# Position products of a disentangled attention: two thirds of them moved to two 64-row tiles of TensorE

## The reference

```python
c2p = jnp.einsum('bhsd,hkd->bhsk', q, pos_k)
c2p = jnp.take_along_axis(c2p, clip(rel + span), axis=-1)
p2c = jnp.einsum('bhsd,hkd->bhsk', k, pos_q)
p2c = jnp.take_along_axis(p2c, clip(-rel + span), axis=-1)
scores = scores + c2p / bias_scale + p2c.swapaxes(-1, -2) / bias_scale
```

## Time and profile before

| | |
|---|---|
| median of 3 executions | 1429.16 us (1428.75 to 1429.78) |
| the profiled execution | 1423.23 us |
| its span in the trace | 1421.4 us |
| prelude's first fill to first `t1` | 428.40 to 445.47 us |
| the 31 units with fills | 445.47 to 1186.44 us |
| one unit in the middle | 23.75 us |
| TensorE busy in that unit | 23.28 us |
| VectorE, ScalarE, GpSimd busy in it | 18.54, 15.01 and 11.14 us |

### The profile page before, as it was taken

The page is one execution under the profiler, slowest core; times in us unless marked ns, Lnnn a source line. Parts: engine busy times, 40 slices in busy tenths (PEclk is TensorE's granted clock), DMA queues, the critical chain, the costliest instruction groups (busy, mean ns, idle before and its releaser), DMA issues. The chain is left out here.

```text
span 1421.4 us, 31237 instructions
## 1 busy us (share of the span) xinstructions
PE 1111.4 (78%) x9281; PEld 990.6 (70%) x9281; DVE 963.6 (68%) x2968; ACT 698.2 (49%) x1449; POOL 553.3 (39%) x418
## 2 busy tenths in 40 slices
PE   4990521885617999999999999999999998730886
PEld 3980411885406898989898989888888886620886
DVE  6887742665635877777777777777777776630564
ACT  2435410443534666666666666666666664210443
POOL 0007135553003444444444444444444443026454
PEclk9995555998668999999999999999999999655999
DMA  5900053223198355555565555555555540043221
GB/s 142 228 15 0 1 195 113 77 78 99 41 312 202 103 142 136 142 134 141 135 139 137 139 137 138 138 138 138 134 142 136 140 111 1 1 162 106 64 80 50
DMA packets 75273, 165.91 MB, mean 117 GB/s; under 512 B 8249, under 2 KB 54784, under 8 KB 66528
## 3 DMA queue, kind: packets, MB, share of 16 engines
q1 hardware_dynamic: 69600, 152.75, 42.0%
q0 software_dynamic: 5632, 12.67, 2.6%
HBM read 130.76 MB, written 35.67 MB: 117 GB/s over the span
## 5 line engine op out<-in xcount | busy, mean ns | idle before, releaser
L1143 POOL TENSOR_SCALAR ds_scores<-ds_scores,ds_max 128x256 f32<-128x256 f32 x256 | 349.0, 1363 | 393.0 <-DVE ds_max L1335 392.9
L1327 DVE TENSOR_TENSOR ds_p2c<-ds_bank,ds_p2c 128x512 f32<-128x512 f32 x256 | 175.8, 687 | 93.1 <-PE ds_bank L1180 93.1
L1276 ACT ACTIVATE all_xt<-ds_bank 128x512 f32<-128x512 f32 x256 | 153.0, 598 | 148.2 <-PE ds_bank L1198 148.2
L1171 PE MATMUL ds_bank<-ds_qr,ds_tab 128*128 128x128 f32 x1536 | 190.2, 278 | 32.2 <-DVE ds_qr L1311 30.0
L1171 PEld LDWEIGHTS ds_bank<-ds_qr,ds_tab 128*128 128x128 f32 x1536 | 181.9, 194 | 33.4 <-issue 33.3
L1171 PE MATMUL ds_bank<-ds_kr,ds_tab 128*128 128x128 f32 x1536 | 197.7, 275 | 0.6 <-ACT ds_p2c L1260 0.6
L1260 ACT ACTIVATE ds_c2p_t<-ds_bank 128x512 f32<-128x512 f32 x256 | 152.7, 597 | 88.6 <-PE ds_bank L1171 87.4
L1335 DVE CUSTOM_DVE_ANT_0 ds_scores<-ds_bank,ds_p2c 128x256 f32<-128x256 f32 x512 | 195.2, 417 | 0.2 <-DVE ds_p2c L1327 0.2
L1171 PEld LDWEIGHTS ds_bank<-ds_kr,ds_tab 128*128 128x128 f32 x1536 | 184.0, 192 | 1.2 <-issue 1.1
L1260 ACT ACTIVATE ds_p2c<-ds_bank 128x512 f32<-128x512 f32 x256 | 149.3, 597 | 53.4 <-PE ds_bank L1171 53.3
L1180 PE MATMUL ds_bank<-all_constants,ds_c2p_t 128*128 128x128 f32 x1024 | 157.6, 276 | 0.0
(11 more groups left out here) (245 smaller groups left out, 1746.7 us busy)
## 6 DMA issues: line engine op xcount, KB each, us to landing
ds_qr<-scratch_qk SPq DMA_DIRECT2D x32, 1024.0 KB, 11.2
ds_kr<-scratch_qk SPq DMA_DIRECT2D x32, 1024.0 KB, 13.9
ds_tab<-scratch_tables SPq DMA_DIRECT2D x64, 248.0 KB, 9.2
slots_in<-all_zero SPq DMA_DIRECT2D x2, 5160.0 KB, 38.0
ds_qs<-scratch_q_parts SPq DMA_DIRECT2D x32, 288.0 KB
ds_ks<-scratch_k_parts SPq DMA_DIRECT2D x32, 288.0 KB
0fe_xb<-slots_in SPq DMA_DIRECT2D x40, 129.0 KB, 2.1
1fe_xb<-slots_in SPq DMA_DIRECT2D x40, 129.0 KB, 2.1
```

Of the source, the lines that this page charges most:

```text
L1143: pool.tensor_scalar(S[b % NS][:, 1, :], S[b % NS][:, 1, :], mx[:, 2 * b + 1:2 * b + 2], None, ALU.subtract).then_inc(s_sub1, 1)
L1171: last = pe.matmul(pb[n % 2][:, a * P:(a + 1) * P], TAB[half][:, kind, c:c + P], mov[:, :].rearrange("p (b g s) -> p g b s", b=HALF, s=16) ...
L1276: act.activation(PT[b], pt2[:, :].rearrange("p (k s) -> p k s", k=2), ACT.Exp).then_inc(s_exp, 1)
L1327: dve.tensor_tensor(z, pt1[b % 2][:, :].rearrange("p (a k) -> p a k", a=2), z, ALU.add).then_inc(s_z, 1)
```

## The change

The twelve near fills become six double fills, each of two banks. A matmul for side 0 and group g uses the same table columns as one for side 1 and group g + 8. For `RUNS` 1 and 2 of each kind (four of the six double fills) these two are done together: for each of the 4 groups, tile 0 takes partitions 0 to 63 of the table and of the moving operand, with places 8 to 15 of both groups, tile 1 partitions 64 to 127 with places 0 to 7. Each has 2 x 8 x 8 = 128 moving columns. Tile 0 writes to bank 0, tile 1 to bank 1. The number of fp32 matmuls stays 4 x 2 = 8 in such a double fill. The third run of each kind pairs groups whose columns differ, and is done with the whole array as before. Below, P is a double fill in two row tiles and F one with the whole array.

A double fill waits until the copies of all earlier fills are done, where before the last one could be open. ScalarE copies a P with four copies of 256 columns, in runs of 8 elements, where there were two of 512 columns in runs of 16. `SHARE` is 1, 1, 1, 1, 1, 1, 2, 2: steps 0 to 5 have P, P, F, P, P, F, steps 6 and 7 two far fills each. `CONTENT_FILLS` goes from 13 to 14.

```diff
-        FILLS = near[:10] + [far[0], near[10], far[1], near[11], far[2], far[3]]
-        CONTENT_FILLS = 1 + max(n for n, f in enumerate(FILLS) if f[0] == 0)
+        RUNS = (((0, 0, 4), (1, 8, 4)), ((0, 4, 4), (1, 12, 4)), ((0, 8, 4), (1, 4, 4)))
+        FILLS = [("near", kind, runs) for kind in range(2) for runs in RUNS] + \
+                [("far", kind, (0, QUADS - 1)) for kind in range(2)] + [("far", kind, (1, 0)) for kind in range(2)]
+        FILLS = FILLS[:6] + [FILLS[6], FILLS[8], FILLS[7], FILLS[9]]
+        BANKS = [2 if f[0] == "near" else 1 for f in FILLS]
+        FIRST = [sum(BANKS[:n]) for n in range(len(FILLS))]
+        BM = sum(BANKS)
+        CONTENT_FILLS = FIRST[8]
-        SHARE = [2, 2, 2, 1, 2, 2, 2, 3]
+        SHARE = [1, 1, 1, 1, 1, 1, 2, 2]
...
-                pe.wait_ge(s_be, f + 1)
+                pe.wait_ge(s_be, f + BANKS[n])
...
+                if where[1][1] != where[0][1] + 8:
+                    for r, (side, grp, _) in enumerate(where):
+                        for a in range(4):
+                            c = TABLE - SEQ + P * side - 16 * (grp + a)
+                            last = pe.matmul(pb[r][:, a * P:(a + 1) * P], TAB[half][:, kind, c:c + P],
+                                             mov[:, :].rearrange("p (b g s) -> p g b s", b=HALF, s=16)[:, grp + a, :, :], start=True, stop=True)
+                        last.then_inc(s_bm, 1)
+                    return
+                side, grp, _ = where[0]
                 for a in range(4):
+                    c = TABLE - SEQ + P * side - 16 * (grp + a)
+                    for tile in range(2):
+                        rows = slice(tile * 64, (tile + 1) * 64)
+                        own = mov[rows, :].rearrange("p (b q g h s) -> p h q g b s", b=HALF, q=2, h=2, s=8)[:, 1 - tile, :, grp + a, :, :]
+                        last = pe.matmul(pb[tile][:, :].rearrange("p (r a n) -> p r a n", r=2, a=4)[:, :, a, :], TAB[half][rows, kind, c:c + P],
+                                         own, start=True, stop=True)
+                        if a == 3:
+                            last.then_inc(s_bm, 1)
...
+                for tile in range(2):
+                    act.wait_ge(s_bm, done + tile + 1)
+                    at = 0
+                    for side, grp, count in where:
+                        dst = to[:, side, :, :].rearrange("p b (g h s) -> p h g b s", h=2, s=8)[:, 1 - tile, grp:grp + count, :, :]
+                        last = act.activation(dst, pb[tile][:, at * 64:(at + count) * 64].rearrange("p (g b s) -> p g b s", g=count, b=HALF), ACT.Copy)
+                        at += count
+                    last.then_inc(s_be, 1)
```

More of the change, by code:

```diff
@@ L1152, in fill @@
             def fill(head, half, n):
-                kind, quad, side = FILLS[n]
-                f = (2 * head + half) * BM + n
+                what, kind, where = FILLS[n]
+                f = (2 * head + half) * BM + FIRST[n]
                 if n == 0:
@@ L1159, in fill @@
                 pe.wait_ge(s_masked, 2 * (2 * head + half) + kind + 1)
-                pe.wait_ge(s_be, f + 1)
+                pe.wait_ge(s_be, f + BANKS[n])
                 mov = (QR, KR)[kind][half]
-                if is_far(quad, side):
+                if what == "far":
+                    side, quad = where
                     pe.wait_ge(s_stack[half], 16 * 4 * (head + 1))
-                    pe.matmul(pb[n % 2][:, :], ENDS[half][:, kind, side * FAR:(side + 1) * FAR],
+                    pe.matmul(pb[FIRST[n] % 2][:, :], ENDS[half][:, kind, side * FAR:(side + 1) * FAR],
                               (QS, KS)[kind][half][:, :].rearrange("p (b s) -> p b s", b=HALF)[:, :, quad * 64:(quad + 1) * 64],
@@ L1167, in fill @@
                     return
-                for a in range(4):
[L1169 to L1174, removed]
+                if where[1][1] != where[0][1] + 8:
[7 more added lines that the diff above has]
+                side, grp, _ = where[0]
+                for a in range(4):
+                    c = TABLE - SEQ + P * side - 16 * (grp + a)
[6 more added lines that the diff above has]
+                            last.then_inc(s_bm, 1)
             def t1(step, half, b):
@@ L1240, in _ @@
             pe.sem_inc(s_av, 2)
-            for n in range(BM):
+            for n in range(len(FILLS)):
                 fill(0, 0, n)
@@ L1252, in copy @@
             def copy(head, half, n):
[L1253 to L1260, removed]
+                what, kind, where = FILLS[n]
+                done = (2 * head + half) * BM + FIRST[n]
+                to = (CT, PC)[kind][half]
+                if what == "far":
+                    side, quad = where
+                    act.wait_ge(s_bm, done + 1)
+                    act.activation(to[:, side, :, quad * 64:(quad + 1) * 64], pb[FIRST[n] % 2][:, :].rearrange("p (b s) -> p b s", b=HALF),
+                                   ACT.Copy).then_inc(s_be, 1)
+                    return
+                if where[1][1] != where[0][1] + 8:
+                    for r, (side, grp, count) in enumerate(where):
+                        act.wait_ge(s_bm, done + r + 1)
+                        dst = to[:, side, :, :].rearrange("p b (g s) -> p g b s", s=16)[:, grp:grp + count, :, :]
+                        act.activation(dst, pb[r][:, :].rearrange("p (g b s) -> p g b s", g=count, b=HALF), ACT.Copy).then_inc(s_be, 1)
+                    return
+                for tile in range(2):
[6 more added lines that the diff above has]
+                    last.then_inc(s_be, 1)
             def head_values(head, half):
```

## The result

The changed kernel took 1357.1 us (median of 4 runs, 1353.68 to 1362.82), the kernel before 1428.95 beside it (1421.65 to 1429.78): a ratio of 0.950, with an interval of 0.948 to 0.953. The profiled execution is the one of 1353.68.

The account below looks back on a forecast made before the run. TensorE's pace was taken as the bound, a unit's saving counting 31 times. 23.75 - 3.58 - 0.47 + 1.25 + 0.34 = 21.29 us a unit, less 1 us for the prelude, gave a 1354 us median, range 1325 to 1405.

Parts of the forecast that it names:

- the forecast case: Whole kernel: the summed terms hold, 1354 us as a median, own range 1335 to 1372; chance 0.55.
- Step 1: TensorE's four P in a unit: two tiles work side by side, 0.89 us each, 3.58 us saved a unit.
- Step 2: TensorE going to and from row tiles: 0.20 us in, 0.15 out, 1.25 us added a unit.
- within 0.8 us: Sign in the trace: a P's 16 instruction starts in step 0 of a unit lie this close if tiles overlap.
- Rival A: In the P, the tiles take turns at 1.79 us each, so the kernel gets slower: 1459 us; chance 0.15.
- Rival D: At the changes of tiling: they are hidden, 1.25 us less a unit, 1315 us; chance 0.06.
- Step 3: ScalarE's copies of a P: both banks must be free before the next double fill, 0.34 us of waits a unit.
- Rival C: ScalarE's short copies cost what long ones do, 2.55 us more a unit, 1433 us; chance 0.04.
- Step 4: Far fills, two each in steps 6 and 7 of a unit: 0.16 us of wait left, 0.47 won.
- Step 5: Order of kinds, `CONTENT_FILLS` and the release of loads: no cost.
- the prelude: Ahead of the loop: six double fills in turn with their copies make it end 1 us later.
- Rival B: VectorE becomes the bound from step 6 to step 1, losing 1 us a unit, 1385 us; chance 0.20.

Follow-up runs that it names:

- e3: Changed kernel with tile 1's matmuls of every double fill left out after the first head, copies kept: 1358.95 us in one run.
- e4: Changed kernel with the P of steps 3 and 4 of a unit cut in two, `t2` between the halves: 1381.76 us in one run.
- e5: Changed kernel with ScalarE's wait for VectorE's last sums moved from a unit's start to just ahead of the first copy: 1349.65 us, 0.947.
- e6: Changed kernel with one of the two short copies of each tile left out after the first head: 1341.13 us in one run.
- e9: Changed kernel with a double fill starting when bank 0 is free, waiting for bank 1 only ahead of its first matmul there: 1349.74 us, 0.949.
- e1: Changed kernel with its order and double fills, but all six with the whole array and no tiles: 1406.72 us, 0.985.
- e8: Kernel before the change with only `SHARE` set to 2 in all eight steps: 1409.35 us, 0.988.
- e10: Changed kernel with e9's waits bank by bank and e5's later ScalarE wait together: 1342.3 us, 0.942.
- e2: Changed kernel with all of tile 0's matmuls of a double fill ahead of all of tile 1's in the program: 1407.42 us in one run.
- e12: Changed kernel with the two F of a unit in row tiles too, 64 moving columns each: 1375.88 us in one run.

## Why the prediction was right

It named 1354 for 1357.1, inside its range, and the forecast case is the one that came true. By its steps:

- **What bounds the kernel.** TensorE's pace, and 31 times what a unit gives: right. A unit of the middle got shorter by 2.23, and 31 x 2.23 = 69, as the loop's 69.4. That the two agree so closely is in part luck: the first unit gave 4.9 and the other 30 gave 2.15 each, since three of them wait for a load.
- **Step 1, two tiles at once.** 8 x 0.1117 = 0.89 predicted for the two tiles together, and that is what they cost. The measured 0.89 from the first start to the last is another sum: seven rounds of 0.112 and 0.10 more in the first one, which step 2 books under going in. The "within 0.8 us" of the prediction's last part had left that 0.10 out. e3 shows that the second tile is free. Rival A (1459) is refuted. The bound taken was the one nearest to the row of `av`.
- **Step 2, changing the tiling.** 0.20 in and 0.15 out predicted, 0.19 and 0.15 measured, 1.22 for 1.25. Rival D, where they are hidden, is refuted by the gaps of the changed kernel and by e4.
- **Step 3, the copies.** This is the term of the sum that was mis-sized, by a factor of two: 0.34 predicted, 0.69 measured. Its wait at step 2 was nearly right, 0.21 where 0.26 stood, but by two errors against each other. The copies begin 0.31 behind a P's last start and not 0.20, since the two tiles end together. And their pitch is 0.27 (four in 1.21) and not 0.33. The 0.33 came from a row that was misread: one of the three copies in 1.68 us had to wait for its far fill, which began only at 828.89, so its (1.68 - 0.596) / 2 = 0.54 is no pitch. Two copies that really follow each other, at 794.46 in the changed kernel's row, stand 1.08 - 0.60 = 0.48 apart. Rival C is refuted. Two things were missing. At the start of a unit ScalarE is held by VectorE: this cost 0.15 in step 0 and, together with the copies' length, 0.13 in step 1, shown by e5 and e6. And a fill whose wait ends only as it is reached gets its weights late, 0.10 for each F, gone in e9.
- **Step 4, the far fills.** 0.47 won predicted, 0.55 measured, since only 0.08 of wait was left for 0.16; this wait too was worked out with the 0.54. e1 and e8 show this gain by itself, 0.56 and 0.65 a unit.
- **Step 5, no cost; the prelude.** 1 us predicted, 3.5 measured. The working took 2.7 for a double fill, from full clock; from start to start the first two P and the F took 3.5, 3.4 and 4.5 at a granted clock of 0.50, and 2.5 from there on.
- **The sum.** 21.29 a unit predicted, 21.52 measured, and 2.5 more for the prelude: together some 9.6 us too little time. In the medians 3 of it is left: the stages around it came out 3.9 shorter in the profiled execution, and that lay 3.4 under its median where 5.93 was added. That part of the nearness is luck.
- **Rival B, VectorE.** Half right: VectorE did come in, at the place named (the mask in step 6, felt in steps 0 and 1), but through ScalarE's order rather than as the bound, and for 0.25 a unit instead of 1. In e10, with 18.2 of 20.86 busy, it still keeps up where its loads are there.

Left open: why single loads take long. That they now matter follows from the shorter unit. In e10 the load of a `QR` is issued 6.8 us into a unit and its mask is reached 18.9 us into it; five loads took 12.3 to 13.7 us to land and came late, the others 9.4 to 11.9. In the kernel before the loads took as long (9.3 to 12.9), and behind the first unit each landed some 2 us or more ahead of its mask. What makes one load take 13 us and the next 10 the traces don't show, and no run tried it.

## What to carry to other kernels

Two row tiles pay where both halves use the same stationary columns and their instructions alternate in the program; price each visit to another tiling as a term of its own, and put visits next to work that is tiled already. When one engine gets faster, look at what its neighbour does ahead of the step that it now needs sooner: a wait that stands at the head of a block rather than just before the instruction that needs it cost 0.25 us a unit here (21.52 to 21.27), and the trace of the kernel before has no wait that showed it. And look at how the work is spread over the steps before a new instruction form: eight numbers gave a quarter of this gain.

## What the runs showed that was not expected

- At full granted clock two instructions in different row tiles start 4 to 7 ns apart, and matmuls of another tile start ahead of earlier ones in the program, by about three (e2).
- With 64 moving columns a round of fp32 matmuls takes the same 0.112 us as with 128 (e12).
- ScalarE's copies that follow each other overlap by some 0.12 us, whatever their width: those of 256 columns last 0.39 and follow at 0.27, those of 512 last 0.60 and follow at 0.48.
- The first fp32 matmul behind a wait that has just ended lasts 377 ns and not 275, and its second starts 0.10 later (the F of steps 2 and 5; in e9 and e6, where no wait ends just there, it is gone).
- A VectorE subtraction of 0.34 us lasted 6.07 beside GpSimd's operation of 9.96 us, and ended 0.15 after it.
